# Post-layernorm block, one core: variances by ScalarE squares, inputs laid out per partition, rests of the weights from PE products

## The reference, cut to what matters

```python
v = x @ W_write.T
inter/intra reads over chunks of 64, with decays gamma ** (distance)
y = x + alpha * (reads @ W_read.T)
x1 = layernorm(x + y)                       # (x - mean) / sqrt(var + 1e-5)
gate, up = fp4_linear(x1, w_gate), fp4_linear(x1, w_up)
out = layernorm(x1 + fp4_linear(silu(gate) * up, w_down))
```

## Time and profile before

| | |
|---|---|
| time, median of 3 runs | 349.37 us (349.29 to 349.79) |
| the profiled execution's own time | 349.22 us |
| its span, first to last instruction | 347.5 us |
| mean granted clock of PE | 0.985 |
| ACT busy | 178.7 us (51%) |
| POOL busy | 242.8 us (70%) |
| DMA | 15.61 MB, 13,611 packets |

### The profile page before, as it was taken

How to read it: one execution, slowest core, us unless ns; L and a number is a source line. 1 busy time by engine, 2 the same in 40 slices (tenths; PEclk the granted TensorE clock), 3 DMA queues, 4 the chain that set the end, 5 groups by cost and what they waited for, 6 DMA issues and landing times.

```text
span 347.5 us, 7092 instructions
## 1 busy us (share of the span) xinstructions
PE 314.8 (91%) x2234; PEld 305.2 (88%) x2234; DVE 319.5 (92%) x806; ACT 178.7 (51%) x378; POOL 242.8 (70%) x261
## 2 busy tenths in 40 slices
PE   0595787989999999999999999999999999999883
PEld 0384777979999999999999999999999999999883
DVE  1789898999999999999999999999999999999994
ACT  3534454644555555535554556554555445545453
POOL 1579595675767668967787678668785785676653
PEclk9987899999999999999999999999999999999999
DMA  5810300030002200040003100210020000000002
GB/s 178 262 51 3 121 0 0 3 121 4 0 17 75 80 17 15 16 138 17 0 15 116 50 0 15 91 60 16 16 78 2 15 15 17 18 15 3 30 31 77
DMA packets 13611, 15.61 MB, mean 45 GB/s; under 512 B 1168, under 2 KB 11280, under 8 KB 13584
## 3 DMA queue, kind: packets, MB, share of 16 engines
q1 hardware_dynamic: 13296, 15.27, 13.4%
q10 hardware_dynamic: 288, 0.00, 0.0%
HBM read 11.08 MB, written 4.19 MB: 44 GB/s over the span
## 4 chain that ended last, share of the span: by engine, by line
PE 53%; DVE 30%; issue 9%; POOL 2%; DMA 2%; ACT 2%; SPq 1%; DVEq 0%; POOLq 0%; ACTq 0%
PE bank L1529 9%; PE bank L1531 9%; PE bank L1530 9%; PE gu L1529 7%; PE gu L1530 7%; PE gu L1531 7%; DVE h_y L928 4%; PE bank L1603 4%; DVE h_g L933 3%; DVE h_am L1054 3%; DVE w_raw L1047 3%; DVE hqT_lo L1075 2%; DMA w_raw<-in_L_ffn_w_up_dram 2%; DVE pr L975 1%; DVE h_rs L923 1%
## 5 line engine op out<-in xcount | busy, mean ns | idle before, releaser
L1529 PE MATMUL gu<-guT_hi,xqT_hi 128*128 128x352 f32 x256 | 85.0, 332 | 1.0 <-DVE w_raw L1047 0.9
L1530 PE MATMUL gu<-guT_lo,xqT_hi 128*128 128x352 f32 x256 | 82.9, 324 | 0.0
L1531 PE MATMUL gu<-guT_hi,xqT_lo 128*128 128x352 f32 x256 | 82.8, 323 | 0.0
L403 POOL TENSOR_TENSOR h_q<-h_g,h_ns 128x704 f32<-128x704 f32 x32 | 46.2, 1443 | 34.3 <-DVE h_g L933 34.3
L1529 PEld LDWEIGHTS gu<-guT_hi,xqT_hi 128*128 128x128 f32 x256 | 48.2, 188 | 2.1 <-DVE w_raw L1047 1.3
L632 ACT ACTIVATE w_raw<-gu 128x352 f32<-128x352 f32 x64 | 29.6, 462 | 37.5 <-PE gu L1531 37.3
L1530 PEld LDWEIGHTS gu<-guT_lo,xqT_hi 128*128 128x128 f32 x256 | 48.2, 188 | 0.0
L1531 PEld LDWEIGHTS gu<-guT_hi,xqT_lo 128*128 128x128 f32 x256 | 48.0, 188 | 0.0
L396 POOL TENSOR_TENSOR h_n<-w_raw,h_rs 128x704 f32<-128x704 f32 x32 | 44.6, 1393 | 4.1 <-DVE h_rs L923 4.0
L1530 PE MATMUL bank<-dnT_lo,hqT_hi 128*128 128x256 f32 x160 | 45.2, 282 | 0.0
L1531 PE MATMUL bank<-dnT_hi,hqT_lo 128*128 128x256 f32 x160 | 45.2, 282 | 0.0
(11 more groups left out here) (111 smaller groups left out, 900.4 us busy)
## 6 DMA issues: line engine op xcount, KB each, us to landing
x_full<-attn_out_transposed_dram SPq DMA_DIRECT2D x8, 512.0 KB, 4.2
xs<-in_L_attn_out_dram SPq DMA_DIRECT2D x8, 512.0 KB, 3.5
out_dram<-wq_gu SPq DMA_DIRECT2D x32, 128.0 KB, 1.7
w_raw<-in_L_ffn_w_down_dram SPq DMA_DIRECT2D x1, 704.0 KB, 9.1
w_raw<-in_L_ffn_w_gate_dram SPq DMA_DIRECT2D x1, 640.0 KB, 7.0
w_raw<-in_L_ffn_w_up_dram SPq DMA_DIRECT2D x1, 640.0 KB, 7.9
wrT<-n_W_read_transposed_dram SPq DMA_DIRECT2D x1, 256.0 KB, 6.2
ww<-in_L_attn_W_write_dram SPq DMA_DIRECT2D x1, 256.0 KB, 7.8
```

The lines of the kernel that those rows point to most:

```text
L403: nc.gpsimd.tensor_tensor(blocks(h_q[:, p, 0:I]), blocks(h_g[:, p, :]), per_block(h_ns[:, p, :], HB), ALU.mult).then_inc(h_quant, 1)
L1529: nc.tensor.matmul(dst, lh, rh, start=(first and i == 0), stop=False)
L1530: nc.tensor.matmul(dst, lh, rl, start=False, stop=False)
L1531: last = nc.tensor.matmul(dst, ll, rh, start=False, stop=(i == len(terms) - 1))
```

## The change

**Variances.** The residual is written with a sum over each row of the tile (`accum_out`); ACT computes (sum - 256 z)^2 with a sum over the row; DVE makes minus the mean and variance + eps from the two sums. The statistics and aggregates go, and with them `x_stats` and `out_stats`. The residual of x is two instructions per pair of tiles instead of one.

```diff
-                nc.vector.scalar_tensor_tensor(
-                    z[:, 2 * u:2 * u + 2, :].rearrange("p i d -> p (i d)"),
-                    xs[:, 2 * u:2 * u + 2, :].rearrange("p i d -> p (i d)"), 2.0, r_bank[u][:], ALU.mult,
-                    ALU.add).then_inc(z_ready, 1)
-            def x_stats(n, u):
-                dve.wait_ge(z_ready, 2 * n + u + 1)
-                for i in (2 * u, 2 * u + 1):
-                    nc.vector.bn_stats(z_bn[:, i, :], z[:, i, :]).then_inc(z_stats, 1)
+                for q in range(2):
+                    i = 2 * u + q
+                    last = nc.vector.scalar_tensor_tensor(z[:, i, :], xs[:, i, :], 2.0, r_bank[u][:, q * D:(q + 1) * D],
+                                                          ALU.mult, ALU.add, accum_out=z_sum[:, i:i + 1])
+                last.then_inc(z_ready, 1)
...
             def x_moments(n, u):
-                for i in (2 * u, 2 * u + 1):
-                    dve.wait_ge(z_stats, 4 * n + i + 1)
-                    nc.vector.nop(nofuse=True)
-                    nc.vector.bn_aggr(z_mv[:, i, :], z_bn[:, i, :]).then_inc(z_moments, 1)
-                dve.wait_ge(z_moments, 4 * n + 2 * u + 2)
-                nc.vector.tensor_scalar(z_nm[:, c], z_mv[:, c, 0], -1.0, None, ALU.mult)
-                nc.vector.tensor_scalar(z_ve[:, c], z_mv[:, c, 1], LN_EPS, None, ALU.add).then_inc(z_var, 1)
+                dve.wait_ge(z_dev, 2 * n + u + 1)
+                nc.vector.tensor_scalar(z_nm[:, c], z_sum[:, c], -1.0 / D, None, ALU.mult)
+                nc.vector.tensor_scalar(z_ve[:, c], z_ssq[:, c], 1.0 / D ** 3, LN_EPS, ALU.mult,
+                                        ALU.add).then_inc(z_var, 1)
...
+            def x_deviations(n, u):
+                act.wait_ge(z_ready, 2 * n + u + 1)
+                for i in (2 * u, 2 * u + 1):
+                    last = nc.scalar.activation(z_off[:, i, :], z[:, i, :], ACT.Square, bias=z_sum[:, i:i + 1],
+                                                scale=-float(D), accum_out=z_ssq[:, i:i + 1])
+                last.then_inc(z_dev, 1)
...
-                nc.vector.tensor_tensor(o_z[:, t % 2, :], x1[:, par, t, :], d_bank[t][:, 0:D],
-                                        ALU.add).then_inc(o_ready, 1)
+                nc.vector.scalar_tensor_tensor(o_z[:, p, :], d_bank[t][:, 0:D], 1.0, x1[:, par, t, :], ALU.mult, ALU.add,
+                                               accum_out=o_sum[:, p:p + 1]).then_inc(o_ready, 1)
```

```diff
+            def w_subtract(f):
+                tiles, hi, _ = w_fill(f)
+                pe.wait_ge(wT_hi_ready, f + 1)
+                nc.tensor.matmul(w_bank[f][:, 0:P * len(tiles)], neg_ident[:], hi, start=False, stop=True,
+                                 skip_group_check=True).then_inc(wT_left, 1)
...
+            def w_remainder(f):
+                tiles, _, lo = w_fill(f)
+                act.wait_ge(wT_left, f + 1)
+                last = nc.scalar.copy(lo, w_bank[f][:, 0:P * len(tiles)])
+                if f == FILLS - 1:
+                    last = nc.scalar.copy(dnT_hi[TAIL:P, HC - 1, :], w_bank[f][TAIL:P, D:2 * D])
+                last.then_inc(wT_lo_ready, 1)
...
-            def w_rest(f):
-                tiles, hi, lo = w_fill(f)
-                dve.wait_ge(wT_hi_ready, f + 1)
-                nc.vector.tensor_tensor(lo, w_bank[f][:, 0:P * len(tiles)], hi.bitcast(F32),
-                                        ALU.subtract).then_inc(wT_lo_ready, 1)
...
+            nc.vector.tensor_scalar(neg_ident[:], ident[:], -1.0, None, ALU.mult)
```

```diff
+            load_w(0)
+            sp.dma_start(x_full[:].rearrange("p c t -> p (c t)"), xt_rows[0]).then_inc(xt_loaded, 16)
+            load_w(1)
+            sp.dma_start(w_pair[:].rearrange("p m c d -> p (m c d)"), w_attn).then_inc(wrw_loaded, 16)
+            load_w(2)
+            load_w(3)
+            sp.dma_start(xs[:].rearrange("p i d -> p (i d)"), x_rows[0]).then_inc(x_loaded, 16)
+            load_w(4)
+            load_w(5)
```

**Order.** The lists of all engines and the banks are new. `combine` has a bank that the first scores don't use. Before the first `gate_up`, PE's list now has all scores, values and reads of batch 1:

```diff
             combine([])
-            scores(0, 0, [(comb_ready, 1)])
+            scores(0, 0, [])
             scores(0, 1, [])
+            w_transpose(0, [])
+            w_transpose(1, [])
...
+            w_subtract(2)
+            w_subtract(3)
+            w_subtract(4)
+            reads(1, 0, [(v_lo_ready, 3)])
+            w_subtract(5)
+            xq_transpose(0, 0, [(v_lo_ready, 4)])
+            reads(1, 1, [(wT_lo_ready, 3)])
             pe.wait_ge(wT_lo_ready, 6)
             gate_up(0, 0, 0, 0, reused=False)
             gate_up(0, 0, 0, 1, reused=False)
-            reads(1, 0, [(pr_ready, 7)])
-            scores(1, 3, [(pr_ready, 5)])
```

More of the change, by code:

```diff
@@ new lines, in body @@
+                x_dequant(n - 1, 1)
+                h_dequant(k - 1, 1)
+                h_normalise(k, 0)
+                out_rstd(k - 4, 0)
+                p_rest(n, 2)
+                x_rstd(n, 0)
+                x_rest(n + 1, 0)
+                x_rest(n + 1, 1)
+                p_rest(n, 3)
+                h_dequant(k, 0)
+                x_normalise(n, 1 - par, 0)
+                h_normalise(k + 1, 1)
+                out_rstd(k - 3, 1)
+            run(pool, body)
+            x_dequant(6, 0)
@@ L1710, in body @@
[L1710 to L1714 removed]
+                scores(n - 1, 3, [(pr_ready, 4 * n - 1)])
+                reads(n - 1, 0, [(v_lo_ready, 2 * n - 1)])
+                gate_up(k - 3, b - 1, 1, 1)
+                xq_transpose(n - 2, 1, [(z_ready, 2 * n - 1)])
@@ new lines, in body @@
+                h_transpose(k - 6, 2, 1, [(pr_ready, k + 4)])
+                values(n - 1, 1, [(o_ready, 4 * n - 10)])
+                gate_up(k - 2, b - 1, 2, 0)
+                down(k - 6, 2, [(hT_lo_ready, 2 * k - 10)])
+                h_transpose(k - 5, 3, 0, [(hT_lo_ready, 2 * k - 11)])
+                h_transpose(k - 5, 3, 1, [(xqT_lo_ready, 2 * n - 2)])
+                gate_up(k - 2, b - 1, 2, 1)
+                reads(n - 1, 1, [(hT_lo_ready, 8 * n - 17)])
+                scores(n, 0, [(v_lo_ready, 2 * n)])
@@ L1743, in _ @@
-            h_transpose(20, 0, 0, [(hT_lo_ready, 39)])
+            run(pe, body)
+            gate_up(21, 5, 1, 1)
+            xq_transpose(5, 1, [(v_lo_ready, 13)])
+            h_transpose(18, 2, 1, [(pr_ready, 27)])
+            values(6, 1, [(o_ready, 18)])
+            reads(6, 0, [(xqT_lo_ready, 12)])
+            scores(6, 3, [(hT_lo_ready, 38)])
+            gate_up(22, 5, 2, 0)
+            h_transpose(19, 3, 0, [(hT_lo_ready, 37)])
+            down(18, 2, [(pr_ready, 28)])
+            h_transpose(19, 3, 1, [(z_ready, 13)])
@@ L1758, in _ @@
-            h_transpose(22, 2, 0, [(pr_ready, 30)])
+            h_transpose(21, 1, 1, [(xqT_lo_ready, 13)])
+            down(20, 0, [(hT_lo_ready, 42)])
+            scores(7, 3, [(pr_ready, 31)])
+            h_transpose(22, 2, 0, [(hT_lo_ready, 43)])
+            values(7, 0, [(o_ready, 21)])
+            h_transpose(22, 2, 1, [(pr_ready, 32)])
             gate_up(25, 6, 1, 0)
-            xq_transpose(6, 1, [(pr_ready, 31)])
+            reads(7, 0, [(v_lo_ready, 15)])
+            down(21, 1, [(hT_lo_ready, 44)])
```

1247 lines of the change are left out of this document (600 added, 647 removed).

## The result

The changed kernel takes 340.29 us (339.71 to 340.89, four runs); the kernel before, on the same chip, 349.58 (349.29 to 350.66). The ratio is 0.973, 95% interval 0.970 to 0.976: 9.3 us less, where 6.1 were forecast. The profiled execution took 340.89 us, with a span of 339.2. The four runs lie in two pairs, at 339.7 and 339.8 and at 340.8 and 340.9 us, and the profiled one is the slowest of them.

A forecast was written before the change was run, and what follows sets the result against it. PE bounds 100 to 250 us; in the start and towards the end DVE is the busier. Span 347.5 + 2.0 - 6.3 - 2.0 + 0.2 = 341.4, so time 343.1 us; range 337.5 to 348.0.

The forecast's parts named there:

- its own case: Whole kernel: the forecast's own band of times, 340.5 to 346 us, around 343.1, given a chance of 0.50.
- start, up to 60 us: Up to 60 us: first gate/up at 47.5, unused PE time 20.4 instead of 27.5, then 3.8 instead of 3.0; gain 6.3 us.
- 60 to 100: From 60 to 100 us: DVE has less to do, PE three products more and less filler; 0 (-2 to +1).
- loop: Loop: same products issued, a batch costs PE 37.25 us as before; 0 (-0.5 to +2 over four batches).
- end, last tile included: From 250 to 335 us DVE's relief gains 2.0 of 3.3 unused; last tile's trip through ACT costs 0.2.
- nine products: PE: nine products of the negative identity with rounded weights, six ahead of the first gate/up; 2.0 us added.
- The late attention weights: Start: one load holding both attention weights, last of 1,728 KB, lands at 12.0 us instead of 10.0; costless if POOL's rests are last.
- An edit that frees DVE brings nothing in it: From 100 to 250 us: PE is busy 150.00 of 150 us, so relieving DVE gains nothing there.
- the prediction's own sign: Loop: the forecast is wrong there if the chain distance between batches is over 37.6 us.
- The small gain: Rival, 347.4 us: DVE's shed work collides with nothing, chains decide first gate/up; gain 3 there, 1 at end; chance 0.20.
- The slower case: Rival, 351.5 us: in the loop DVE's queue stops for ACT's squares, slower from 0.94 us per step; chance 0.07.
- The large gain: Rival, 338.4 us: free sum writes, full clock, first gate/up at 43.8; startup 10, end 3; under 340.5, chance 0.19.

The follow-up runs named there:

- written-out kernel: The changed kernel with the two rounds of its loop written out one after the other, nothing else: 336.84 us, ratio to before 0.9635.
- the kernel before with the new loads: The kernel before with only its loads changed (one piece per partition, weights by unit, the changed kernel's order of loads): 345.93 us, ratio 0.990.
- the order alone: The changed kernel with variances (statistics apart) and rests of the weights back on DVE, leaving new loads and order: 357.24 us, against 345.9 for old order, same loads.

## Why the prediction was right, and where not

The time was 2.8 us under the forecast, inside its range (337.5 to 348.0) and just under the lower edge of its own case (340.5). The sum was nearly right with terms that were not.

| term, us | forecast | profile after |
|---|---|---|
| start, up to 60 us | -6.3 | -8.2 |
| 60 to 100 | 0 | -2.1 |
| loop | 0 | +3.6 |
| end, last tile included | -1.8 | -2.9 |
| nine products | +2.0 | +1.2 by the count, the rest in the rows above |

**Start.** The first gate/up was to come at 47.5; it came at 47.38, with 20.9 us unused ahead of it where 20.4 were forecast. The size that was off is what follows: up to 60 us 3.8 were to be unused, and it was 1.7; the filler that I took as used up was not missed. That stretch and the next (0 forecast, -2.1 measured) hold most of what the time was under the forecast. The clock fell between 30 and 37 us before; the same window now:

```profile
30.00:37.00 7.00, 7.00 (x51) 6.70 (x52) 5.33 (x19) 4.02 (x12) 6.57 (x7) 1.00 0.41 142
```

51 matmuls instead of 25, at the upper level (2.4 GHz). It did not decide: in the written-out kernel the mean from 10 to 46.4 us was 0.95 instead of 1.00, and its first gate/up came at 47.25. (The clock's rows don't tell all of it: from 15.3 to 19.3 us the changed kernel's 512-column matmuls start 0.43 us apart, the written-out one's 0.23, and both rows read 1.00.)

What stands last ahead of the first gate/up is PE's own list, as forecast. PE last waits for DVE at 39.87 us; from there its matmuls follow each other to 47.38, and DVE's rest of quantised x is done at 46.67:

```profile
45.98 0.69 DVE L1078 TENSOR_TENSOR xqT_lo<-bank,xqT_hi 128x512 fp32r<-128x512 f32 x1 [0.63 <-ACT xqT_hi L639]
```

```profile
47.27 0.28 PE L1528 MATMUL bank<-v_hi,pr_lo 128*128 128x256 f32 x1
47.38 0.32 PE L1526 MATMUL gu<-guT_hi,xqT_hi 128*128 128x352 f32 x1
```

The forecast had DVE there at 42.6 plus what collisions cost. It came 4.1 us after that and is only 0.7 ahead of PE, so with 4 us of rests back on it, gate/up comes 2.3 later. That the time met 47.5 to 0.1 us is in part luck, since the forecast also counted on a clock that falls, and between 30 and 37 us it did not. Of the 9.3 us the loads alone give 3.6, of which the forecast knew the 2.3 of DVE's wait.

**The late attention weights** did not come. I had them at 12.0, last of 1,728 KB at the 288 GB/s of the earlier trace rows; they landed at 9.8, and PE started on them at 9.92. The step that failed is taking the old pieces' rate for the new ones. The rates of the first 20 us, a slice each half microsecond, of the changed kernel and then of the one before:

```profile
GB/s 0 0 0 0 23 57 175 197 258 103 172 374 389 392 431 399 417 414 399 422 428 411 417 406 385 389 270 135 11 0 0 0 82 246 352 360 8 0 0 0
```

```profile
GB/s 0 0 0 0 60 60 160 297 154 129 164 182 301 336 381 395 354 299 297 311 290 319 303 346 381 383 375 375 302 224 182 84 27 51 197 377 385 41 0 0
```

From 6 to 10 us, 389 to 431 now and 297 to 395 before; the kernel before with the new loads has 377 to 433. The late load cost nothing either way, since the scores wait for POOL (15.32 us; forecast 16).

**Loop.** "An edit that frees DVE brings nothing in it" is right for the order before: there the variances on ACT left 1099 matmuls of 1105. It is wrong for the order that the change brings. With statistics on DVE this order gives PE only 1074 matmuls in 150 us, so there the relief is worth 3.8 us, and 13.2 to 13.8 over the whole run. The forecast's 0 for the batch distance was right (37.33), but as the sum of an order that costs and a relief that pays. The stall at the jump was in no term; it costs 2.3 to 3.45 us and stands in no trace of the old loop. By the prediction's own sign (a batch distance over 37.6 us) it was wrong in the loop: two batches took 39.2 each in the mean.

**End.** The relief was to give 2.0 of 3.3. It gives 7.5 against the same order without it, and 1.1 in the old order. The last tile was priced at +0.2. From the last residual to the last normalisation there are now 2.28 us (334.05 to 336.33), before 2.34: the square, 0.49, and the trip are as long as statistics and aggregate were.

```profile
334.05 0.42 DVE L1124 SCALAR_TENSOR_TENSOR wq_gu<-bank,x 128x256 f32<-128x256 f32 x1 [0.93 <-PE bank L1528]
...
334.40 0.08 DVE L1124 DVE_READ_ACCUMULATOR wq_gu<-bank,x 128x1 f32 x1
334.57 0.49 ACT L670 ACTIVATE o_off<-wq_gu,o_sum 128x256 f32<-128x256 f32 x1
334.97 0.19 ACT L670 ACTIVATION_READ_ACCUMULATOR o_off<-wq_gu,o_sum 128x1 f32 x1
335.19 0.15 DVE L1130 TENSOR_SCALAR o_nm<-o_sum 128x1 f32<-128x1 f32 x1 [0.70 <-ACT o_off L670]
```

**DVE and ACT.** DVE was to fall to 286 and stands at 295.3. The sums are as taken, 64 rows of 0.084 us, 5.4 us in all for a forecast of 5. The Trainium skill ("VectorE: DVE Perf Modes", Two Vector instructions with no wait between them) counts them as instructions of their own; the trace agrees, and shows the same on ACT, at 0.19 us each. What was missed is what other steps lose: `z_nm` takes 491 ns in the mean where it took 287, `z_ve` 327 instead of 161, 5.8 us together. The rest is spread over many rows, most of them a few tenths longer, and 4.2 us of rise come with the order alone (318.4 to 322.7 above). Why the operations are longer the runs don't show; with the squares made twice `z_nm` took 233. ACT's 214.3 is the forecast's 215, in part by luck: the squares have 0.51 us (0.484 taken) and their 64 sums 12.2 us for which nothing was added, but these rows overlap, and busy time is their union. In the old order squares and sums together make ACT busy for 31.0 us more (178.4 to 209.3), the forecast's number.

```profile
L1049 DVE TENSOR_SCALAR z_nm<-z_sum 128x2 f32<-128x2 f32 x16 | 7.8, 491 | 2.5 <-ACT z_off L625 2.4
...
L1050 DVE TENSOR_SCALAR z_ve<-z_ssq 128x2 f32<-128x2 f32 x16 | 5.2, 327 | 0.0
...
L1124 DVE DVE_READ_ACCUMULATOR wq_gu<-bank,x 128x1 f32 x32 | 2.7, 84 | 0.0
```

**Rivals.** The small gain (what DVE sheds collides with nothing, a gain of 3 in the start) did not come: the start gave 8.2, and in the new order the shed operations are worth 13.2 and 6.6 us. In the old order, by contrast, the variances on ACT cost 1.9. The slower case (DVE stopping for ACT's squares) did not come, since at 0.51 + 0.19 us per square the waits sum to 3.9 us. Its price was too low: it was to make the kernel slower than before from 0.94 us of waiting at each step, but with the squares made twice 0.35 on average already leave it 5.8 us slower. The forecast let DVE's 4.6 free us per batch absorb the first 0.77 us of each wait; the loop lost 1.3 us per batch all the same. That a wait in the chain isn't absorbed is my reading, not shown: ACT's other work was late as well. The margin is thin. The large gain (under 340.5) is where the time fell, but its reason, a first gate/up at 43.8, did not come; with the stall gone (336.8) the kernel is below the whole range.

## What to carry to other kernels

A reordering and a relief cannot be priced one after the other: here the order alone costs 11.3 us, one of its two reliefs alone, in the old order, costs 1.9, and all together bring 5.6 beyond the loads. So "this engine has slack, the edit brings nothing" holds only for the order whose trace shows it. And look for "issue" where a list jumps back; one trace had 3 us there, a forecast by counts of work does not see it, and writing the loop out removed it.

## What the runs showed of the hardware

- DVE's list stood still for 2.0 and 1.0 us behind a jump, beside four fetches of 8 KB in 10 us; writing the loop out gave 3.45 us, of which up to 1.2 are not the stall's. The same loop body in a kernel with nine more DVE operations ahead of it had no such gap; twenty no-ops ahead of it did not remove it. Not settled.
- One piece per partition and load, with the order of loads that goes with it (8,240 packets in the run instead of 13,611), moved 389 to 431 GB/s from 6 to 10 us, and 377 to 433 in the kernel before with these loads, against 297 to 395 before. Pieces and order were not tried apart.
- A gap of PE of 2.2 us, with work on both sides, was followed by 3.2 us at the lower clock (0.50 granted from 162.8 to 166.0).
